# One VectorE maximum over both PSUM banks in place of one for each bank, in a softmax-routed layer on one core

## What is computed, cut to what matters here

```
xn     = layernorm(x)
logits = (xn @ phi_w.T + phi_b).reshape(t, z, 64, 32)      # experts n, slots p
D      = softmax(logits, axis=3)                           # over the slots of one expert
C      = softmax(logits, axis=2)                           # over the experts of one slot
X_tilde= einsum('tznp,tzd->npd', D, xn)                    # summed over every token
Y      = einsum('tznp,npH->tzH', C, expert(X_tilde))
x      = x + attention(xn) * silu(Y)
# then a second layer: a recurrence and a gated block on the new x
```

## Time and profile before

| | us |
|---|---|
| median of 3 runs | 1187.49 |
| lowest, highest | 1187.18, 1188.07 |
| span of the profiled execution | 1184.2 |

### The profile page before, as it was taken

The page is one execution under the profiler, slowest core; times in us unless marked ns, Lnnn a source line. Parts: engine busy times, 40 slices in busy tenths (PEclk is TensorE's granted clock), DMA queues, the critical chain, the costliest instruction groups (busy, mean ns, idle before and its releaser), DMA issues. The chain is left out here.

```text
span 1184.2 us, 17639 instructions
## 1 busy us (share of the span) xinstructions
PE 1144.7 (97%) x5097; PEld 787.9 (67%) x5097; DVE 1050.1 (89%) x1608; ACT 981.7 (83%) x2128; POOL 958.9 (81%) x770
## 2 busy tenths in 40 slices
PE   5999999999999999999989999999999999999996
PEld 3666666565666666666457777777777777777764
DVE  7999999999999999999767888888888888888887
ACT  5877877877766766766668999999999999999998
POOL 3998999898999999999788777878777788877751
PEclk9999999999999999999999999999999999999999
DMA  4445435434424432443754444344444444444420
GB/s 131 152 152 200 141 140 182 153 128 164 155 109 160 155 133 113 161 156 129 225 188 154 131 142 143 119 147 128 142 143 143 131 128 134 141 128 142 142 72 18
DMA packets 125263, 167.36 MB, mean 141 GB/s; under 512 B 7536, under 2 KB 102000, under 8 KB 125040
## 3 DMA queue, kind: packets, MB, share of 16 engines
q1 hardware_dynamic: 123984, 165.71, 41.4%
q10 hardware_dynamic: 1184, 0.53, 0.2%
HBM read 90.71 MB, written 75.50 MB: 140 GB/s over the span
## 5 line engine op out<-in xcount | busy, mean ns | idle before, releaser
L146 POOL TENSOR_TENSOR exp_slots_loaded<-exp_slots_loaded,slot_max 128x1024 f32<-128x1024 f32 x128 | 323.2, 2545 | 6.6 <-DMA exp_slots_loaded<-exp_slots 3.2
L858 POOL TENSOR_TENSOR dd<-ed,rz 128x512 f32<-128x512 f32 x256 | 267.6, 1051 | 24.7 <-ACT rz L688 23.4
L563 PE MATMUL acc<-dd,xns 128*128 128x512 f32 x512 | 261.1, 592 | 0.7 <-POOL dd L858 0.7
L1917 DVE TENSOR_TENSOR clo<-ct,chi 128x512 fp32r<-128x512 f32 x256 | 171.5, 681 | 24.3 <-ACT chi L1585 21.6
L176 POOL TENSOR_TENSOR ch<-exp_slots_loaded 128x512 f32<-128x512 f32 x128 | 165.9, 1296 | 32.0 <-ACT exp_slots_loaded L666 30.9
L795 DVE TENSOR_REDUCE mr<-lg 128x16 fp32r<-128x512 f32 x256 | 168.0, 685 | 19.3 <-PE lg L506 16.9
L657 ACT ACTIVATE ed<-lg 128x512 f32<-128x512 f32 x256 | 145.6, 594 | 40.3 <-PE lg L540 38.4
L666 ACT ACTIVATE exp_slots_loaded<-lg 128x512 f32<-128x512 f32 x256 | 145.5, 594 | 26.4 <-PE lg L549 24.4
L1585 ACT ACTIVATE chi<-ct 128x512 fp32r<-128x512 f32 x256 | 147.7, 597 | 11.8 <-PE ct L1219 8.3
L1219 PE MATMUL ct<-identity,exp_slots_loaded 128*128 128x128 f32 x1024 | 150.9, 273 | 5.6 <-POOL exp_slots_loaded L146 3.1
L811 DVE TENSOR_REDUCE zd<-ed 128x32 f32<-128x1024 f32 x128 | 154.6, 1208 | 1.5 <-ACT ed L657 1.5
(11 more groups left out here) (315 smaller groups left out, 2500.2 us busy)
## 6 DMA issues: line engine op xcount, KB each, us to landing
exp_slots<-exp_slots_loaded SPq DMA_DIRECT2D x128, 512.0 KB, 3.4
exp_slots_loaded<-exp_slots SPq DMA_DIRECT2D x128, 512.0 KB, 3.5
xns<-xn_rows SPq DMA_DIRECT2D x128, 64.0 KB, 1.9
b_xraw<-in_xT SPq DMA_DIRECT2D x16, 256.0 KB, 3.8
out_t<-b_ti SPq DMA_DIRECT2D x15, 256.0 KB, 2.1
expert_w_late<-in_expert_w SPq DMA_DIRECT2D x5, 512.0 KB, 11.1
xn_rows<-slot_sum SPq DMA_DIRECT2D x8, 256.0 KB, 2.5
expert_w_early<-in_expert_w SPq DMA_DIRECT2D x3, 512.0 KB, 5.8
```

The source lines that it names most:

```text
L146: e.tensor_tensor(rows, rows, joined(SM, b)[:, h].unsqueeze(2).broadcast_to([P, TPB, GC * EPC, NP]), ALU.mult).then_inc(s_we)
L563: e.matmul(acc[k][:, :], xns[v % RX][:, :], dd[v % RX][:, bank(k)], start=tile == 0, stop=tile == NT - 1, skip_group_check=True).then_inc( ...
L858: e.tensor_tensor(dd[v % RX][:, bank(k)].rearrange("q (n p) -> q n p", p=NP), ed[v % RD][:, bank(k)].rearrange("q (n p) -> q n p", p=NP), ...
L1917: e.tensor_tensor(clo[g % RC][:, :], ct[c % 2][:, :], hi_f32(chi[g % RC][:, :]), ALU.subtract).then_inc(c_l)
```

## The change

`expert_max` becomes one instruction for each unit. It reads both banks of `lg` and writes 32 columns of `mr`. It waits until both banks' logits are there; before, the first of the two instructions waited for bank 0 alone. The transpose waits for two maxima for each unit in place of three (`MX`), and so does ScalarE's `shift_kept`.

```diff
-            MX = 3
+            MX = 2
...
-                def expert_max(i, r, k):
+                def expert_max(i, r):
                     v = unit(i, r)
                     if v is not None:
-                        e.wait_ge(s_l, 2 * v + k + 1)
-                        e.tensor_reduce(mr[v % 2][:, k * HN // 2:(k + 1) * HN // 2], lg[v % 2][:, bank(k)].rearrange("q (n p) -> q n p", p=NP),
-                                        AX_X, ALU.max).then_inc(s_mx)
+                        e.wait_ge(s_l, 2 * (v + 1))
+                        e.tensor_reduce(mr[v % 2][:, 0:HN], lg[v % 2][:, :].rearrange("q (n p) -> q n p", p=NP), AX_X,
+                                        ALU.max).then_inc(s_mx)
...
-                    expert_max(i - 1, 1, 0)
-                    expert_max(i - 1, 1, 1)
+                    expert_max(i - 1, 1)
                     slot_max(i - 1, 1)
```

More of the change, by code:

```diff
@@ L826, in vector1 @@
                     minus_mean(i)
-                    expert_max(i - 1, 1, 0)
-                    expert_max(i - 1, 1, 1)
+                    expert_max(i - 1, 1)
                     slot_max(i - 1, 1)
                     expert_sum(i - 1, 0)
-                    expert_max(i - 1, 2, 0)
-                    expert_max(i - 1, 2, 1)
+                    expert_max(i - 1, 2)
                     slot_max(i - 1, 2)
@@ L835, in vector1 @@
                     slot_sums(i - 2)
-                    expert_max(i - 1, 3, 0)
-                    expert_max(i - 1, 3, 1)
+                    expert_max(i - 1, 3)
                     slot_max(i - 1, 3)
@@ L840, in vector1 @@
                     expert_sum(i - 1, 2)
-                    expert_max(i, 0, 0)
-                    expert_max(i, 0, 1)
+                    expert_max(i, 0)
                     slot_max(i, 0)
```

## The result

| | before | after | forecast |
|---|---|---|---|
| median | 1187.51 us | 1203.79 us | 1200.3 (1194.0 to 1206.0) |
| lowest, highest | 1187.18, 1188.07 | 1203.48, 1204.55 | |
| ratio to before | | 1.0139, 95% interval 1.0125 to 1.0154 | 1.0108 |

The change costs 16.3 us (the kernel before has a median of 1187.51 us here from four executions, and had 1187.49 from the three on record before). It is slower, as forecast, and by 3.5 us more than forecast.

A forecast was written before the change was run, and what follows sets the result against it. The prediction took a loop between VectorE and TensorE to set late turns, VectorE to bound early ones; added waits of 0.4 + 2.1 + 2.3 + 8.0 = 12.8 us take 1187.49 to 1200.3 us, range 1194.0 to 1206.0.

The forecast's parts named there:

- r0 and r1 covered: In turns 17 to 32, TensorE's other work hides the merged maximum's delay: 0.27 us at r0, 0.53 at r1.
- covered, with 0.25 us left: Unit r1, turns 17 to 32: slot_max ends at 460.89, TensorE's transpose is due at about 461.2 us.
- Late turns: Turns 17 to 32: r2's uncovered wait lengthens each from 16.96 to 17.49 us, 15 x 0.53 = 8.0 us.
- r0's cover of 0.03 us: Unit r0, turns 17 to 32: transpose ready at 456.50, TensorE turns to r1's logits at 456.47; counted as nothing.
- Early turns: Turns 2 to 12: the loop through r0 and r2 takes 17.81 against 17.60 us, 10 x 0.21 = 2.1 us.
- Turns 12 to 17: Five turns between the two regimes: one at 0.2 us, four at 0.53 us, 2.3 us in all.
- The start-up: The two turns before 47.61 us, given the price of turns 2 to 12: 0.4 us.
- VectorE keeps its win: Rival: VectorE bounds turns 2 to 12 and finds both banks ready, -2.9 us, 1184.6 us or 1180.1; chance 0.05.
- the early turns win: Rival: turns 2 to 12 gain, turns 17 to 32 lose; -2.9 + 2.1 + 8.0 = +7.2, 1194.7 us; chance 0.13.
- Cancelled: Rival: TensorE partly makes up its waits in turns 17 to 32; sum within 2 us, 1187.5 us; chance 0.06.
- Two units pay: Rival: a second unit's delay also counts, 1.06 us in turns 17 to 32, 0.42 in 2 to 12; 1212.8 us; chance 0.08.

The follow-up runs named there:

- merge_r2: The kernel before with only r2's two maxima merged; r0, r1 and r3 keep one for each bank: 1197.75 us, ratio 1.0083.
- waits_only: The kernel before with nothing merged: still one maximum for each bank, but both wait for both banks' logits; 1207.21 us, ratio 1.0152.
- merge_r0: The kernel before with only r0's two maxima merged: 1191.65 us, ratio 1.0028.
- merge_r1_r3: The kernel before with r1's and r3's maxima merged, r0's and r2's not: 1192.60 us, ratio 1.0035.
- merge_r3: The kernel before with only r3's two maxima merged: 1186.51 us, ratio 0.9999.
- bias_shifted_more: The kernel before with an extra unused VectorE sum over 512 elements ahead of turn 12's two small bias instructions: 1188.19 us, ratio 1.0015.
- bias_shifted: The kernel before with an extra unused VectorE sum over 256 elements ahead of turn 12's two small bias instructions: 1187.30 us, ratio 1.0007.

## Why the prediction was right, and where it was off

**The direction and the mechanism were right.** The wait for bank 1 was named as what the change adds, 0.53 us as its size and r2 as the place where TensorE waits. merge_r2 shows 17.50 us for a late turn against 17.49, and the full change 17.53. The 0.06 us a unit for the merge also held: waits_only lies 0.12 us a turn above the change, for two merged maxima on the loop. The nearness of the total does not rest on errors that cancel: all four stretches lost more than forecast.

**r0 and r1 covered: right for r0, half right for r1.** merge_r0 adds 0.03 us to a late turn, as worked out. For r1 I had looked only at the transpose that reads it. Its 0.29 us a turn (merge_r1_r3 less merge_r3) come by way of VectorE's list. In the full change that is hidden behind r2's wait, so the sum was not harmed, but the step "covered, with 0.25 us left" was incomplete. It was also too generous: in the trace of before the product of r1's transpose starts at 461.24, and with the 0.06 + 0.17 us used for r0 behind 460.89 that leaves 0.12.

**Late turns: 8.0 against 8.5.** The missing 0.04 us a turn: the merged maximum takes 1.14 us from start to start after a wait (475.66 - 474.52), not 1.13, and r0's cover of 0.03 us is just overrun.

**Early turns: 2.1 against 3.0.** The step that was mis-sized is the stretch between the merged r0 and the end of r2's logits. VectorE's side went as told: r1 starts 184.76 - 179.66 = 5.10 us after r0 (forecast 5.20). TensorE's weight loads of the changed kernel in that stretch show what was not in the working:

```profile
185.47 0.19 PEld L549 LDWEIGHTS lg<-shift_experts_to_slots,mt 128*128 128x128 f32 x1 [0.85 <-ACT ed L657]
```

TensorE waits there for ScalarE's exponentials of r0, 0.85 us of idle loads, where it was 0.59 in the kernel before. r2's logits then end at 187.94 + 0.39 = 188.33, which is 8.67 after r0's start in place of 8.62, though the transpose of r1 was on time. ScalarE takes its instructions in order, and ahead of the second of these exponentials stands the logarithm of VectorE's expert sum of the unit before, which the merged r0 has put off: it starts at 184.21, after 0.16 us of idle released by L811, where in the kernel before it had not to wait. This is read from the trace; no run of its own tested it. The other 0.04 us are the start-to-start distance of 1.14 (0.01), the hand-over to the transpose's load at 190.78 (0.01) and 6.74 in place of 6.72 us to the end of r0's next logits (0.02): 190.78 - 179.66 = 11.12, and 11.12 + 6.74 + 0.04 = 17.90.

**Turns 12 to 17: 2.3 against 3.8.** Of the five, turn 12 alone lost 19.49 - 17.99 = 1.50 where 0.21 was given. 1.1 of it is the stall of L326 behind GpSimd's half sum. The other four lost 0.54, 0.46, 0.80 and 0.46 where 0.53 was given; the 0.80 was not followed up.

**The start-up: 0.4 against 1.0** cannot be judged. The slot sum of turn 2 starts at 47.82 us in merge_r3, 48.08 in bias_shifted_more, 46.98 in bias_shifted and 47.61 in the kernel before, though the turns before it hold the same work in all four but for r3's merge in the first.

**The rivals.** "VectorE keeps its win" and "the early turns win" fall: the early turns lost 0.30 us each. "Cancelled" falls with merge_r2. "Two units pay" falls for late turns: r0 pays 0.03. (Its price was added up loosely: 1.06 a late turn and 0.42 an early one give 15.9 + 5.0 + 4.7 = 25.6, not 25.3.)

**Rule against row.** The rule of the Trainium skill in the prediction, by the estimate made there 125 ns for each VectorE instruction with a PSUM source ("VectorE: DVE Perf Modes", the section on the TRN2 errata), would have had the merge give back twice what it did. The measured value is 0.06 us for each merge whose time counts, since neighbours overlap. The same page's advice ("Rules for kernel authors") to minimize the count of operations cost 16 us here, since the larger operation has to wait for more.

## What to carry to other kernels

Merge instructions only where the data of the last part is there when the engine arrives (r3 here); where it is not, the earlier part ran while the last part's data was still being made, and the merge puts that run time behind the wait: 0.53 us lost at such a place here, against 0.06 saved elsewhere. To price a delay, follow it on both roads, to the engine that waits for the result and down the delayed engine's own list, and expect the delays of several places to overlap rather than add. An engine with 100% busy time can still sit on a loop with another: exchanging two TensorE instructions shortened turns in which VectorE was full, from 17.60 to 17.48 us.

## What was not expected of the hardware

A VectorE `tensor_scalar` from SBUF to SBUF on 128x8 elements takes 0.17 us, and 1.16 to 1.30 us when a GpSimd `tensor_tensor` on SBUF starts 0.01 to 0.22 us ahead of it; 0.01 or 0.05 us the other way round it takes 0.17. A shift of 0.3 us in VectorE's list so cost 1.1 us in one place here. VectorE's maxima from PSUM follow one another every 1.13 us for 1024 elements and every 0.60 us for 512, though the records last 1.22 and 0.69.
